# A hand-ordered transformer kernel on one core: another order of the steps' work on TensorE, ScalarE and VectorE

## What is computed

```python
def attn_layer(x, Wqkv, qs, ksc, Wo):
    q, k, v = jnp.split(x @ Wqkv, 3, -1)             # 16 heads of 64
    q = l2norm(q) * qs
    k = l2norm(k) * ksc
    q = q * cos * scale + rotate_half(q) * sin * scale
    k = k * cos / scale + rotate_half(k) * sin / scale
    out = local_attention(q, k, v)                   # windows of 32, with the window before
    return out @ Wo
def ffn_layer(x, g, bln, W1, b1, W2, b2):
    xn = (x - mu) / jnp.sqrt(var + 1e-05) * g + bln
    a, gate = jnp.split(xn @ W1 + b1, 2, -1)         # 341 + 341 channels
    return a * jax.nn.gelu(gate, approximate=False) @ W2 + b2
for i in range(6):
    x = attn_layer(shift_tokens(x), Wqkv[i], q_scale[i], k_scale[i], Wo[i]) + x
    x = ffn_layer(shift_tokens(x), ln_g[i], ln_b[i], W1[i], b1[i], W2[i], b2[i]) + x
```

## Time and profile before

| | us |
|---|---|
| median of 3 executions | 2246.75 (2243.56 to 2249.29) |
| the profiled execution | 2244.96 |
| its span (first to last instruction) | 2243.2 |
| TensorE busy | 2034.3 (91%) |
| VectorE busy | 1359.3 (61%) |
| ScalarE busy | 1328.8 (59%) |
| GpSimd busy | 1079.3 (48%) |

### The profile page before, as it was taken

The page is one execution under the profiler, slowest core; times in us unless marked ns, Lnnn a source line. Parts: engine busy times, 40 slices in busy tenths (PEclk is TensorE's granted clock), DMA queues, the critical chain, the costliest instruction groups (busy, mean ns, idle before and its releaser), DMA issues.

```text
span 2243.2 us, 73622 instructions
## 1 busy us (share of the span) xinstructions
PE 2034.3 (91%) x32680; PEld 1198.6 (53%) x32680; DVE 1359.3 (61%) x1663; ACT 1328.8 (59%) x1640; POOL 1079.3 (48%) x708
## 2 busy tenths in 40 slices
PE   8999998779999999999999999999999999999987
PEld 4655655345555555555555555555555555555553
DVE  1444444566666666666766666666676666666662
ACT  4444354365666666656666666666666666666664
POOL 0000000377555555655656555655565656555550
PEclk9999999799999999999999999999999999999999
DMA  3000000022223222232322222222222223222220
GB/s 104 2 1 1 2 19 29 19 58 67 59 60 94 68 68 58 59 87 58 77 59 59 77 68 74 62 58 67 78 75 66 62 59 96 68 67 59 59 58 20
DMA packets 81912, 128.04 MB, mean 57 GB/s; under 512 B 17214, under 2 KB 28092, under 8 KB 81468
## 3 DMA queue, kind: packets, MB, share of 16 engines
q1 hardware_dynamic: 81596, 123.33, 21.2%
HBM read 21.55 MB, written 1.05 MB: 10 GB/s over the span
## 4 chain that ended last, share of the span: by engine, by line
PE 66%; ACT 14%; issue 8%; DVE 7%; POOL 3%; SPq 0%; POOLq 0%; DMA 0%; ACTq 0%; DVEq 0%
PE ps L598 14%; PE ps L624 8%; PE ps L602 7%; PE ps L662 5%; PE ps L679 5%; PE ps L655 5%; ACT KT L962 4%; PE ps L414 4%; PE ps L642 3%; PE ps L607 2%; PE ps L611 2%; DVE work L1055 2%; POOL work L1377 2%; DVE work L1052 2%; ACT ps L953 2%
## 5 line engine op out<-in xcount | busy, mean ns | idle before, releaser
L1377 POOL TENSOR_TENSOR work<-work,RS 128x1024 f32<-128x1024 f32 x192 | 361.6, 1904 | 313.3 <-ACT RS L996 313.3
L602 PEld LDWEIGHTS ps<-ident,work 128*128 128x128 f32 x3072 | 343.6, 142 | 149.3 <-issue 71.0
L1052 DVE TENSOR_TENSOR work<-ps,work 128x1024 f32<-128x1024 f32 x192 | 230.8, 1202 | 311.4 <-ACT work L975 300.0
L602 PE MATMUL ps<-ident,work 128*128 128x128 f32 x3072 | 392.7, 276 | 27.0 <-ACT work L949 12.2
L1371 POOL TENSOR_TENSOR work<-work 128x1024 f32<-128x1024 f32 x96 | 226.2, 2356 | 370.0 <-DVE work L1055 370.0
L598 PE MATMUL ps<-WK,XS 128*128 128x512 f32 x384 | 189.5, 616 | 51.0 <-ACT KT L962 51.0
L1055 DVE TENSOR_TENSOR work<-ps,work 128x1024 f32<-128x1024 f32 x192 | 233.1, 1214 | 0.0
L1091 DVE TENSOR_REDUCE SS<-work 128x16 f32<-128x1024 f32 x192 | 232.1, 1209 | 0.0
L1364 POOL TENSOR_TENSOR work<-work 128x1024 f32<-128x1024 f32 x96 | 226.1, 2355 | 5.7 <-DVE work L1055 5.7
L662 PEld LDWEIGHTS ps<-work 64*32 64x32 f32 x12288 | 136.0, 106 | 163.2 <-issue 106.2
L922 ACT ACTIVATE work<-ps 128x1024 f32<-128x1024 f32 x96 | 98.1, 1022 | 208.7 <-PE ps L662 206.9
(11 more groups left out here) (184 smaller groups left out, 3102.2 us busy)
## 6 DMA issues: line engine op xcount, KB each, us to landing
work<-work SPq DMA_DIRECT2D x576, 128.0 KB
work<-work SPq DMA_DIRECT2D x336, 64.0 KB
WQ<-in_wqkv SPq DMA_DIRECT2D x6, 512.0 KB, 3.6
WK<-in_wqkv SPq DMA_DIRECT2D x6, 512.0 KB, 4.2
WV<-in_wqkv SPq DMA_DIRECT2D x6, 512.0 KB, 3.6
WO<-in_wo SPq DMA_DIRECT2D x6, 512.0 KB, 3.8
work<-ZR SPq DMA_DIRECT2D x48, 64.0 KB
W<-in_w SPq DMA_DIRECT2D x6, 341.0 KB, 3.0
```

The source lines that it names most:

```text
L602: m = nc.tensor.transpose(flat(R)[:, t * 128:t * 128 + 128], src[:, t * 128:t * 128 + 128], ident[:, :])
L1052: V.tensor_tensor(h16(cos_part[:, j, :]), h16(flat(src)), rotary_tabs[:, at:at + 64].unsqueeze(1).broadcast_to([PARTS, 16, 64]), ALU.mult) ...
L1377: U.tensor_tensor(h16(qk_norm[:, j, :]), h16(cos_part[:, j, :]), inv_norms[:, j, :].unsqueeze(2).broadcast_to([PARTS, 16, 64]), ALU.mult). ...
```

## The change

Within a step, the order of the work changes on three engines; in numbers of instructions only one step of the FFN changes hands.

1. TensorE: the heads are turned before the values are projected, and the keys are turned straight after the values. The FFN's and the output projection's piece, which stood between the turned heads and the turned keys, now stands between the turned keys and the turned queries.
2. TensorE at n = 1: chunk 1 of the hidden layer is computed whole ahead of the first half of the weighing; chunk 2's gate half stands between the halves of the weighing and its value half behind them.
3. ScalarE: turned heads are copied before the values; at n = 1 the GELU table is loaded after the copy of the turned keys. `square` (n = 0) still stands ahead of that copy.
4. The FFN's affine step leaves ScalarE: VectorE's `norm` multiplies by the scale in the same instruction and adds the bias in a second one, at the end of step n = 0.
5. VectorE at n = 1: `gated` for chunk 1 moves behind the scores' maximum and shift.

```diff
@@ TensorE, step @@
                     project(bank_z, w_q, 1, n).then_inc(q_projected, 1)
+                if d:
+                    pe.wait_ge(heads_copied, g - 2)
+                    turn(bank_y, heads).then_inc(heads_turned, 1)
                 if b:
                     pe.wait_ge(wv_loaded, 16 * ((g - 1) // 16 + 1))
...
                     m.then_inc(values_ready, 1)
-                if d:
-                    pe.wait_ge(heads_copied, g - 2)
-                    turn(bank_y, heads).then_inc(heads_turned, 1)
+                if b:
+                    pe.wait_ge(k_normed, g)
+                    if d:
+                        pe.wait_ge(heads_turned_copied, g - 2)
+                    turn(bank_y, qk_norm[:, 1, :]).then_inc(k_turned, 1)
                 if f is not None and n == 0:
                     centre(f)
...
                 if b:
-                    pe.wait_ge(k_normed, g)
-                    if d:
-                        pe.wait_ge(heads_turned_copied, g - 2)
-                    turn(bank_y, qk_norm[:, 1, :]).then_inc(k_turned, 1)
                     if a:
                         pe.wait_ge(q_sin, g + 1)
...
                     pe.wait_ge(hidden_gated, 3 * f + 1)
-                    hid_gate(1, bank_f)
+                    hid(1, bank_f)
...
                 if f is not None and n == 1:
-                    hid_value(1, bank_f)
+                    pe.wait_ge(gate_gelu, 3 * f + 2)
+                    hid_gate(2, bank_f)
...
                     pe.wait_ge(hidden_gated, 3 * f + 2)
-                    hid(2, bank_f)
+                    hid_value(2, bank_f)
@@ ScalarE, step @@
-                if f is not None and n == 1:
-                    ffn_affine(f)
...
-                if f is not None and n == 1:
-                    nc.scalar.preload_act_table_set(GELU)
                 if b:
                     act.wait_ge(k_turned, g)
...
                     A(k_t[:, :, 32 + 128 * par:160 + 128 * par], turned(bank_y), ACT.Copy).then_inc(k_turned_copied, 1)
+                if f is not None and n == 1:
+                    nc.scalar.preload_act_table_set(GELU)
+                if b:
                     act.wait_ge(q_turned, g)
@@ VectorE @@
-                V.tensor_tensor(normed[:, :], bank_f[:, 1, :], spread[:, :], ALU.mult).then_inc(ffn_normed, 1)
+                V.scalar_tensor_tensor(out=normed[:, :], in0=bank_f[:, 1, :], scalar=layer_vecs[:, f // 4 * 9 + 6:f // 4 * 9 + 7], in1=spread[:, :], op0=ALU.mult, op1=ALU.mult).then_inc(ffn_normed, 1)
+                dve.wait_ge(ffn_normed, f + 1)
+                V.tensor_scalar(ffn_in[:, :], normed[:, :], layer_vecs[:, f // 4 * 9 + 7:f // 4 * 9 + 8], None, ALU.add).then_inc(ffn_input, 1)
...
-                if f is not None and n == 1:
-                    gated(f, 1, bank_f)
                 if b:
                     dve.wait_ge(scores_ready, g)
...
                     V.tensor_tensor(scores_sb[:, :, :, :], by_head(bank_x), per_head(row_max[:, :]).unsqueeze(3).broadcast_to([PARTS, 8, 2, 64]), ALU.subtract).then_inc(scores_shifted, 1)
+                if f is not None and n == 1:
+                    gated(f, 1, bank_f)
```

More of the change, by code:

```diff
@@ L910, in inverse @@
                 A(spread[:, :], spread[:, :], ACT.Exp, scale=-0.5).then_inc(ffn_inverse, 1)
[L912 to L916, removed]
             def copy_heads(g):
@@ L937, in step @@
                     A(squares[:, 0, :], flat(bank_z), ACT.Square).then_inc(q_squared, 1)
[L938 to L942, removed]
                 if d:
@@ L950, in step @@
                 if b:
+                    act.wait_ge(values_ready, g)
+                    if due(g - 1):
+                        act.wait_ge(windows_loaded, 160 * (g - 1))
+                    A(v_rows[:, (n - 1) % 2, :], flat(bank_x), ACT.Copy).then_inc(values_copied, 1)
+                if b:
                     act.wait_ge(values_copied, g)
@@ L1078, in norm @@
                 if due(f):
-                    dve.wait_ge(ffn_input, f)
-                V.tensor_tensor(normed[:, :], bank_f[:, 1, :], spread[:, :], ALU.mult).then_inc(ffn_normed, 1)
+                    dve.wait_ge(hidden_ready, 3 * f)
+                V.scalar_tensor_tensor(out=normed[:, :], in0=bank_f[:, 1, :], scalar=layer_vecs[:, f // 4 * 9 + 6:f // 4 * 9 + 7], in1=spread[:, :], op0=ALU.mult, op1=ALU.mult).then_inc(ffn_normed, 1)
+                dve.wait_ge(ffn_normed, f + 1)
+                V.tensor_scalar(ffn_in[:, :], normed[:, :], layer_vecs[:, f // 4 * 9 + 7:f // 4 * 9 + 8], None, ALU.add).then_inc(ffn_input, 1)
             def update(f):
```

## The result

| | before | changed |
|---|---|---|
| median us | 2246.49 (4 executions) | 2307.32 (4 executions, 2306.54 to 2312.15) |
| ratio | | 1.0278, 95% interval 1.0262 to 1.0293 |
| span of the profiled execution | 2243.2 | 2304.0 |

What follows compares the result with a forecast made beforehand. TensorE, busy 91% of the span, was taken as the bound, so only its waits could change. Terms of +2.34 us a round over 22 rounds gave +51.5, less 1 before the first FFN: 2296 us, range 2274 to 2310.

Steps and rivals of the forecast that it cites:

- -0.34 and -0.70: At n = 1: keys' projection starts 0.34 us earlier; the wait before the last hidden chunk shrinks, 0.70 us a round.
- +1.86: At n = 2: the keys' turn waits for GpSimd, so the keys' projection starts 1.86 us later.
- `k_normed` keeps its distance from the step's start: End of GpSimd's two products stays 5.39, 5.81, 6.53, 5.36 us after the step's start, n = 0 to 3.
- The handover from GpSimd: From GpSimd's release to TensorE's start: 0.14 us taken, lower bound 0.03, the difference worth 0.4 us a round.
- `square` holds the keys' copy: At n = 0 on ScalarE, `square` stands ahead of the keys' copy; the keys' projection starts 0.93 us later.
- Hidden chunks: At n = 1 on TensorE, the 0.78 us wait before the third chunk goes, some 0.08 remain: -0.70 us a round.
- Affine step: nothing: The addition hides in VectorE's 1.22 us idle at the start of n = 1; uncovered, at most 15 us.
- Heads ahead of values: nothing: Copied values and the windows' transfers come 0.87 us later, but are needed only over 10 us later: no cost.
- The clock: TensorE's dips to 1.2 GHz: rival with one each round, +1.7 us a round, 2335 us, chance 0.08.
- The new waits absorb stalls: Rival: TensorE stalls ahead of the keys' turn become free, -1.26 us a round if all did, 2268 us, chance 0.08.
- The signs: If right: about 2.3 us idle before the keys' turn at n = 2; steps of 17.2, 19.5, 20.0, 18.0 us.
- The faster rival: GpSimd's products are ready when the keys' turn comes up: -3.5 us a round, 2170 us, chance 0.04.

Runs made afterwards that it cites:

- experiments 1 and 2: The changed kernel with the keys' turn back behind the FFN's or output projection's piece: 2220.84 us; the same at n = 2 alone: 2250.10 us.
- experiment 3: The changed kernel with ScalarE's `square` moved behind the copy of the turned keys at n = 0: 2283.89 us.
- experiment 5: The kernel before with only the hidden chunks' new places at n = 1, `gated` for chunk 1 behind the shift: 2223.36 us, ratio 0.9909.
- experiment 6: The kernel before with only the FFN's affine step moved from ScalarE to VectorE: 2228.30 us, ratio 0.9943.
- Experiment 4: The changed kernel with GpSimd's two products in the other order, keys first: 2266.75 us.
- experiment 8: Changed kernel with keys' turn back behind the FFN's piece, `square` behind keys' copy, table load behind queries' copy, n = 3 matmuls cut in two: 2192.31 us.

## Why the prediction was right, step by step

The direction and the mechanism were right: 2307 us in a range of 2274 to 2310, and the waits that the sum is made of are in the trace. In the clean round:

| step | predicted | measured |
|---|---|---|
| n = 0 | +0.93 | 16.26 to 17.15, +0.89 |
| n = 1 | -0.34 and -0.70 | 20.55 to 19.41, -1.14 |
| n = 2 | +1.86 | 18.16 to 19.92, +1.76 |
| n = 3 | +0.59 | 17.40 to 17.93, +0.53 |
| round | +2.34 | +2.04 |

- *`k_normed` keeps its distance from the step's start*: 5.36, 5.92 and 6.52 in the rows above against 5.39, 5.81 and 6.53. This was what the sum rested on, and experiments 1 and 2 show that the wait for it is the loss.
- *The handover from GpSimd*: mis-sized. I took 0.14; it is 1781.35 - 1781.30 = 0.05, near the lower bound of 0.03. That makes the terms of n = 0, 2 and 3 too high, by 0.04 to 0.10. At n = 1 the later `k_normed` ate it: the keys' projection starts at 9.50 us, 0.25 earlier than before and not 0.34, and the back half of that step gained 0.89 and not 0.70.
- *`square` holds the keys' copy*: shown by experiment 3.
- *Hidden chunks*: -0.70 predicted, -0.82 alone in experiment 5 and -0.89 in the changed kernel, so the gain was sized too small.
- *Affine step: nothing*: on the kernel before it is worth 13 to 16 us (experiment 6). In the changed kernel the keys' turn waits for GpSimd and not for ScalarE, so it should bring nothing there; no run shows that by itself.
- *Heads ahead of values: nothing*: 8 us slower by itself.
- *The clock*: here the forecast failed, and in the direction of the total. I put the dips at nothing in the sum and at each round in a rival; they came in 8 of 21 rounds, at the place named (the wait at n = 2) and at 1.69 us each against at most 1.7. A granted clock under 1.00 over the rounds, which I had named as a sign of being wrong, is there: 0.99. The total came out 11 us above the forecast: 10 for dips and 5 unassigned, less the 7 by which 22 rounds of the order were overpriced, make 8 of them. In part it was luck that the time lies inside the range: 2296 with the 15 alone is 2311, just past its end of 2310, and the overpriced order took it back.
- *The new waits absorb stalls*: they did not. Without the dips (0.64 a round) the average round is 1.36 us longer than the clean one, against 1.26 before with its two dips.
- *The signs*: the steps came as named, and the keys' copy at n = 0 too. The idle time ahead of the keys' turn is 2.10, and 0.83, 1.40 and 0.83 at the others, where I had named 2.3 and 1.0 to 1.5: I counted from start to start, and a row counts from the modelled end of the matmuls before, 0.16 later.
- *The faster rival*, that the keys' turn finds its input ready, needed GpSimd to be about 2 us earlier at n = 2. Experiment 4 made it so by a change of GpSimd's order and gained less than the rival's price, since the queries took the wait over.

Still open: what the stalls inside the small matmuls are, and why the dips came in eight rounds and not in the others, which have the same wait.

## What to carry to other kernels

Ahead of a move that frees a late wait, look at how long the input of the moved piece has been ready: here the FFN's piece hid two waits in turn, one for the input ahead of it or one for the copy behind it, and moving it swapped a wait of 0.33 to 0.41 us (1.32 at n = 1, most of it the table load) for one of 0.8 to 2.1. Cut such a filler in two, so that each part is as long as the wait that it covers (experiment 8, n = 3, 0.36 us a round). And reordering the producer can pass the wait to whoever reads or frees its other result, as at two of four steps in experiment 4.

## What I had not expected of the hardware

- A wait of 2.1 us on TensorE between dense matmuls was followed by a stretch of 3.4 us at half the clock in 8 of 21 rounds, while waits of 0.8 and 1.4 us in the same rounds never were. With the 2.1 us wait cut to the 1.1 us of experiment 4 none came at n = 2.
- One instruction less on ScalarE, 0.80 us long, gave 0.67 us a round through the table load behind it (experiment 6): 1.28 us of table load sat on the path, though no row names it as what TensorE waits for.
